# Causal linear attention in front of a mixture of experts: running sums of outer products replaced by chunks of 64 tokens

## What is computed

```python
Q, K, V = (proj(wq_w, wq_b), proj(wk_w, wk_b), proj(wv_w, wv_b))
scores = jnp.einsum('bhld,bhsd->bhls', Q, K)
causal = jnp.tril(jnp.ones((l, l), dtype=scores.dtype))
out = jnp.einsum('bhls,bhsd->bhld', scores * causal, V)
...
x = x + _L0_attn_ref(_layernorm(x, axis=-1), ...)
x = x + _L0_ffn_ref(_layernorm(x, axis=-1), ...)
```

## Time and profile before

| | |
|---|---|
| median of three executions | 309.36 us |
| profiled execution, first to last instruction | 350.7 us (no time outside the span is given for it) |
| busy: TensorE, VectorE, GpSimd, ScalarE | 234.8 (67%), 207.1 (59%), 198.4 (57%), 140.9 us (40%) |
| mean granted TensorE clock | 0.854 |
| chain that ended last | issue 52%, TensorE 27%, DMA 5%, SyncE's queue 4% |

### The profile page before, as it was taken

The page is one execution under the profiler, slowest core; times in us unless marked ns, Lnnn a source line. Parts: engine busy times, 40 slices in busy tenths (PEclk is TensorE's granted clock), DMA queues, the critical chain, the costliest instruction groups (busy, mean ns, idle before and its releaser), DMA issues.

```text
span 350.7 us, 6314 instructions
## 1 busy us (share of the span) xinstructions
PE 234.8 (67%) x1320; PEld 174.7 (50%) x1320; DVE 207.1 (59%) x745; ACT 140.9 (40%) x509; POOL 198.4 (57%) x184
## 2 busy tenths in 40 slices
PE   0799999999998999574300685977677686665000
PEld 0345666666565655363100675976567685554000
DVE  6888887989898989654541043434333443343074
ACT  2434566566565554342200363444343544342000
POOL 3465644588888888744673045554564455646300
PEclk9999999999999999855555599689898989999555
DMA  7910000000010101101121332223223232201199
GB/s 218 304 57 0 3 0 3 3 31 30 31 33 30 33 30 33 53 31 38 39 84 60 72 99 70 71 71 76 68 72 84 62 78 65 81 28 39 50 358 317
DMA packets 32399, 25.48 MB, mean 73 GB/s; under 512 B 4305, under 2 KB 30169, under 8 KB 32364
## 3 DMA queue, kind: packets, MB, share of 16 engines
q1 hardware_dynamic: 23808, 14.52, 15.2%
q0 software_dynamic: 4320, 8.47, 7.6%
q10 hardware_dynamic: 4236, 2.10, 2.0%
HBM read 13.92 MB, written 11.61 MB: 73 GB/s over the span
## 4 chain that ended last, share of the span: by engine, by line
issue 52%; PE 27%; DMA 5%; SPq 4%; ACT 3%; DVE 2%; ACTq 1%; another core or an unknown queue 1%; POOL 1%; DVEq 1%; POOLq 0%
PE ps L824 14%; PE ps L832 9%; PE ps L817 4%; DMA back<-returned 3%; ACT hT L458 3%; SPq L271 2%; SPq L289 2%; DMA bias_bc<-b_o 1%; DMA returned<-y_sb,xt 1%; POOL outer L324 1%; DMA xt<-dispatched 1%; DMA dispatched<-padding 1%; PE ps L709 0%; DVEq L243 0%
## 5 line engine op out<-in xcount | busy, mean ns | idle before, releaser
L349 POOL DMA_INDIRECT returned<-y_sb,xt x71 | 70.2, 988 | 70.9 <-DVE y_sb L685 51.3
L324 POOL TENSOR_TENSOR outer<-qkv 128x1024 f32<-128x1024 f32 x32 | 62.6, 1957 | 32.4 <-ACT qkv L404 32.0
L340 POOL DMA_INDIRECT dispatched<-rows,slot x64 | 62.5, 976 | 25.1 <-issue 15.4
L680 DVE TENSOR_TENSOR yb<-ps,b_bc 128x128 f32<-128x128 f32 x71 | 20.7, 291 | 77.2 <-PE ps L832 32.8
L824 PE MATMUL ps<-xT,w_of 128*128 128x128 f32 x284 | 51.1, 308 | 18.7 <-ACT hT L458 12.5
L739 PE MATMUL ps<-outer,causal 128*128 128x512 f32 x128 | 62.4, 610 | 0.0
L832 PE MATMUL ps<-w_sb,hT 128*128 x284 | 50.0, 304 | 16.3 <-ACT hT L458 10.3
L452 ACT ACTIVATE xT<-ps 128x128 f32<-128x128 f32 x71 | 19.8, 279 | 91.7 <-PE ps L817 72.1
L824 PEld LDWEIGHTS ps<-xT,w_of 128*128 128x128 f32 x284 | 42.8, 216 | 23.0 <-ACT xT L452 16.4
L832 PEld LDWEIGHTS ps<-w_sb,hT 128*128 128x128 f32 x284 | 42.3, 214 | 20.1 <-issue 19.9
L458 ACT ACTIVATE hT<-ps,b_col 128x128 f32<-128x128 f32 x142 | 44.4, 370 | 4.7 <-remote 3.0
(11 more groups left out here) (115 smaller groups left out, 355.5 us busy)
## 6 DMA issues: line engine op xcount, KB each, us to landing
xt<-dispatched SPq DMA_DIRECT2D x71, 65.0 KB
back<-returned SPq DMA_DIRECT2D x8, 512.0 KB, 7.6
x_sb<-x SPq DMA_DIRECT2D x8, 256.0 KB, 5.2
out<-x_sb ACTq DMA_DIRECT2D x8, 256.0 KB, 6.6
returned<-y_sb,xt POOLq DMA_INDIRECT x71, 2.3
w_sb<-w SPq DMA_DIRECT2D x1, 1024.0 KB, 5.6
w_sb<-w SPq DMA_DIRECT2D x2, 512.0 KB, 7.2
dispatched<-rows,slot POOLq DMA_INDIRECT x64
```

The source lines that it names most:

```text
L324: pool.tensor_tensor(outer[:, g % OUTER_RING, :].rearrange("p (h b a) -> p h b a", h=HEADS, b=DH), k, v, ALU.mult).then_inc(outer_done, 1)
L340: pool.indirect_dma_start(out=dispatched[:, :], out_offset=bass.IndirectOffsetOnAxis(ap=slot[:, g * K + k:g * K + k + 1], axis=0), in_=row ...
L349: pool.indirect_dma_start(out=returned[:, :], out_offset=bass.IndirectOffsetOnAxis(ap=xt[:, n % G, D:D + 1].bitcast(I32), axis=0), in_=y_s ...
```

## The change

The attention stage is replaced; the experts' stage and all that follows the count stay as they are.

- Tokens are taken in chunks of 64. Within a chunk the scores are formed and masked, between chunks a state is kept. The norm, both transposes, the projections, the copies and the gate run once a batch of four tiles, output, residual and second norm once for two tiles.
- `project_qk` gives q and k with the features on the partitions, 512 tokens at a time (L771, L773), with one PSUM bank for both; `project_kv` gives k and v with the tokens on the partitions in two halves that share a bank (L783, bias L785). ScalarE copies k (L383) and q (L401), and writes q four more times (L404), each with all but one head of every group of four set to zero (`member`, a 0/1 scale and bias per partition).
- `score_half` (L832): for each half of the heads, four matmuls of k's 32 feature rows and 64 tokens by q's four masked copies, 256 columns, into two partition halves and two banks. VectorE multiplies by the mask of the chunk (`mask_half`, L529, 512 columns).
- `within` (L848): eight matmuls of 64 token rows by 32 features of v, 256 columns. For each head of a group VectorE adds the wanted part (`member_step`, L550, four steps for two tiles, 256 columns).
- `sum_half`, `sum_tile` (L803, L793, L795): the state of each chunk, summed in PSUM; VectorE masks it (`state_out`, L523, 256 columns). `between` (L818): state by q, 64 columns for each chunk, copied by ScalarE (`between_out`, L422) to where the member steps add.
- GpSimd's outer product is gone; the constants that it wrote in its first slot come ahead. `zeros` is new there, and SyncE loads `bias_cols`. The statistics of the first norm move from ahead of VectorE's slots into them. `q_member`, `scores` and `state` lie in the tile `back`, which is otherwise used at the end.

```diff
-
-            def outer_product(g):
-                wait(pool, qkv_done, g + 1)
-                wait(pool, run_done, g + 1 - OUTER_RING)
-                k = heads(qkv[:, g % QKV_RING, D:2 * D]).unsqueeze(2).to_broadcast([P, HEADS, DH, DH])
-                v = heads(qkv[:, g % QKV_RING, 2 * D:3 * D]).unsqueeze(3).to_broadcast([P, HEADS, DH, DH])
-                pool.tensor_tensor(outer[:, g % OUTER_RING, :].rearrange("p (h b a) -> p h b a", h=HEADS, b=DH), k, v,
-                                   ALU.mult).then_inc(outer_done, 1)
...
-            tile_slots([(16, dispatch), (0, outer_product)], N)
+            tile_slots([(12, dispatch)], N)
...
+            def qT_out(g):
+                if g % T:
+                    return
+                b = g // T
+                wait(act, qT_mm, b + 1)
+                wait(act, between_mm, 2 * (b - 1))
+                act.activation(qT[:, b % 2, :], ps_qk, ACT.Identity, bias=bias_cols[:, 0:1]).then_inc(qT_done, 1)
+                act.wait_ge(bias_member_done, 1)
+                for m in range(M):
+                    act.activation(q_member[:, b % 2, m, :], ps_qk, ACT.Identity, bias=bias_member[:, m:m + 1],
+                                   scale=member[:, m:m + 1]).then_inc(qT_done, 1)
...
+            def kv_out(g):
+                if g % T:
+                    return
+                b = g // T
+                wait(act, within_mm, g - T)
+                wait(act, sum_mm, g - T)
+                for half in range(2):
+                    wait(act, kv_mm, 2 * b + half + 1)
+                    act.activation(kv[:, b % 2, 2 * half:2 * half + 2, :], ps_kv, ACT.Identity).then_inc(kv_done, 1)
...
+            def between_out(g):
+                if g % 2:
+                    return
+                wait(act, between_mm, g // 2 + 1)
+                wait(act, att_mm, g // 2 - 3)
+                act.activation(oT[:, g // T % 2, (g % T) * P:(g % T + 2) * P], ps_between, ACT.Identity).then_inc(between_done, 1)
...
-            tile_slots([(10, variance_log2), (12, exponentials), (10, scale2_out), (2, qkv_out), (11, xn2T_out), (1, xnT_out), (6, qT_out), (10, rows_out),
-                        (0, normalize), (7, oT_out), (0, deviations_ahead)], N)
+            tile_slots([(-6, deviation1), (4, deviation2), (-4, xnT_out), (8, exponentials), (1, between_out), (-3, kT_out),
+                        (-3, qT_out), (-2, kv_out), (4, rows_out), (-5, normalize), (7, xn2T_out)], N)
...
+            def state_out(g):
+                first = int(g % T == 0)
+                wait(dve, sum_mm, g + 1)
+                wait(dve, between_mm, g // 2 - 1)
+                dve.tensor_tensor(state[:, g % T, first:2, :], ps_sum[:, g // T % 2, first:2, :],
+                                  headmask[:, :].unsqueeze(1).to_broadcast([P, 2 - first, D]), ALU.mult).then_inc(state_done, 1)
...
+            def mask_half(g, half):
+                wait(dve, scores_mm, 2 * g + half + 1)
+                wait(dve, within_mm, g - 1)
+                dve.tensor_tensor(scores[:, g % 2, half * 2 * M * C:(half + 1) * 2 * M * C].rearrange("p (j m l) -> p j m l", j=2, m=M),
+                                  ps_scores.rearrange("p j (m l) -> p j m l", m=M),
+                                  chunk_causal[:, :].unsqueeze(1).unsqueeze(1).to_broadcast([P, 2, M, C]),
+                                  ALU.mult).then_inc(masked_done, 1)
...
+            def member_step(g, m):
+                if g % 2:
+                    return
+                b, pair = g // T, g // 2
+                if m == 0:
+                    wait(dve, within_mm, g + 2)
+                    wait(dve, between_done, pair + 1)
+                else:
+                    dve.wait_ge(member_out, (M - 1) * pair + m)
+                part = oT[:, b % 2, (g % T) * P:(g % T + 2) * P].rearrange("p (c f) -> p c f", c=2)
+                dve.scalar_tensor_tensor(out=part, in0=ps_o[:, m, :, :, :].rearrange("p c t l -> p c (t l)"), scalar=member[:, m:m + 1], in1=part,
+                                         op0=ALU.mult, op1=ALU.add).then_inc(oT_done if m == M - 1 else member_out, 1)
...
-            def attend(g):
-                wait(dve, run_done, g + 1)
-                wait(dve, qkv_done, g + 1)
-                wait(dve, o_done, g - 1)
-                q = heads(qkv[:, g % QKV_RING, 0:D]).unsqueeze(2).to_broadcast([P, HEADS, DH, DH])
-                run = ps_run[g % 2].rearrange("p u f -> p (u f)").rearrange("p (h b a) -> p h b a", h=HEADS, b=DH)
-                dve.tensor_tensor(prod[:, g % 2, :].rearrange("p (h b a) -> p h b a", h=HEADS, b=DH), run, q,
...
-
-            def attend_sum(g):
-                wait(dve, prod_done, g + 1)
-                wait(dve, oT_mm, g + 1 - RING)
-                dve.tensor_reduce(o_sb[:, g % RING, :], prod[:, g % 2, :].rearrange("p (f a) -> p f a", a=DH),
-                                  AX_X, ALU.add).then_inc(o_done, 1)
...
-            tile_slots([(6, stats2_out), (6, mean2_out), (5, add_residual), (9, softmax_end), (1, attend_sum),
-                        (8, softmax_start), (0, attend), (0, scales_ahead), (9, places), (6, shift2_out),
-                        (2, state_out)], N)
...
+            tile_slots([(11, places), (-5, shift1_out), (-5, constants), (2, member_0), (0, mask_0), (2, member_1), (3, add_residual),
+                        (8, softmax_start), (-6, mean1_out), (2, member_2), (3, stats2_out), (4, shift2_out), (0, mask_1),
+                        (2, member_3), (-1, state_out), (3, mean2_out), (9, softmax_end)], N)
...
+            def project_qk(g):
+                if g % T:
+                    return
+                b = g // T
+                wait(pe, xnT_done, b + 1)
+                wait(pe, between_done, 2 * b - 1)
+                pe.matmul(ps_qk, wqkv_sb[:, D:2 * D], xnT[:, b % 2, :], start=True, stop=True).then_inc(kT_mm, 1)
+                wait(pe, kT_done, b + 1)
+                pe.matmul(ps_qk, wqkv_sb[:, 0:D], xnT[:, b % 2, :], start=True, stop=True).then_inc(qT_mm, 1)
+
+            def project_kv(g):
+                if g % T:
+                    return
+                b = g // T
+                for half in range(2):
+                    wait(pe, kv_done, 2 * b + half)
+                    for u in range(2):
+                        at = 2 * half + u
+                        pe.matmul(ps_kv[:, u, :], xnT[:, b % 2, at * P:(at + 1) * P], wqkv_sb[:, D:3 * D], start=True, stop=False)
+                        wait(pe, bias_done, 4)
+                        mm = pe.matmul(ps_kv[:, u, :], ones[:, :], bias_parts[:, D:3 * D], start=False, stop=True)
+                    mm.then_inc(kv_mm, 1)
...
+            def sum_tile(g):
+                b, u = g // T, g % T
+                if u == 0:
+                    return
+                wait(pe, state_done, g)
+                pe.matmul(ps_sum[:, b % 2, 1, :], kv[C:P, b % 2, u - 1, 0:D], kv[C:P, b % 2, u - 1, D:2 * D],
+                          start=False, stop=True, skip_group_check=True).then_inc(half_mm, 1)
+                pe.matmul(ps_sum[:, b % 2, 0, :], kv[:, b % 2, u - 1, 0:D], kv[:, b % 2, u - 1, D:2 * D],
+                          start=False, stop=True, skip_group_check=True)
+
+            def sum_half(g):
+                b, u = g // T, g % T
+                wait(pe, kv_done, 2 * b + 2)
+                wait(pe, state_done, g)
+                wait(pe, half_mm, (T - 1) * b + u)
+                pe.matmul(ps_sum[:, b % 2, 1, :], kv[0:C, b % 2, u, 0:D], kv[0:C, b % 2, u, D:2 * D],
+                          start=(u == 0), stop=True, skip_group_check=True).then_inc(sum_mm, 1)
+
+            def between(g):
+                if g % 2:
+                    return
+                b = g // T
+                wait(pe, state_done, g + 2)
+                wait(pe, between_done, g // 2)
+                wait(pe, qT_done, (M + 1) * (min(b + 2, B) if g % T else b + 1))
                 for u in range(2):
-                    mm = pe.matmul(ps_run[g % 2][:, u, :], causal[:, :], outer[:, g % OUTER_RING, 512 * u:512 * (u + 1)],
-                                   start=True, stop=True)
-                mm.then_inc(run_done, 1)
...
+                        own = zeros[:, :] if g % T + u + c == 0 else state[:, g % T + u, c, :]
+                        if g == 0:
+                            pe.wait_ge(zeros_done, 1)
+                        mm = pe.matmul(ps_between[:, (2 * c + u) * C:(2 * c + u + 1) * C], own,
+                                       qT[:, b % 2, (g % T + u) * P + c * C:(g % T + u) * P + (c + 1) * C], start=True, stop=True)
+                mm.then_inc(between_mm, 1)
...
+            def score_half(g, half):
+                b, u = g // T, g % T
+                if u == 0:
+                    wait(pe, qT_done, (M + 1) * (b + 1))
+                    wait(pe, kT_done, b + 1)
+                wait(pe, masked_done, 2 * g + half)
+                for c in range(2):
+                    for j in range(2):
```

(25 more changed lines are left out.)

461 lines of the change are left out of this document (237 added, 224 removed).

## The result

The changed kernel takes **545.85 us** (median of four executions, 545.52 to 548.11) against 309.08 for the kernel before beside it: **1.767 times as long, interval 1.763 to 1.772**. The prediction was 480 with a range of 380 to 575. Direction and range held; 66 us are missing, and the sum comes out near by luck: two of its steps were wrong with opposite signs.

The account below looks back on a forecast made before the run. TensorE in the attention stage was taken as the bound. Eight batches of 28.1 us work plus 10.5 us waits give +183 us, start +5, tail -17: +171 on the 309.4 us median, so 480 us, range 380 to 575.

Parts of the forecast that it names:

- What bounds before, and that TensorE would get more work: Attention stage: TensorE, busy 120.9 of 126.1 us, is the bound; its work grows from 15.8 to 28.1 us a batch.
- A group of n then takes n + 1 passes: Scores and within-chunk products: the next small matmul starts only beside the previous one's second pass; 16.3 us a batch.
- the sign that I had set: Small matmuls in the attention stage: the forecast is wrong if their passes are shorter than 0.2 us.
- the rival of full overlap: Small-matmul groups: a group costs only two passes, 5.2 us a batch in all; 391 us, chance 0.20.
- Drain at 0.16 a change: Rival: TensorE waits 0.16 us at each of some 32 array-shape changes a batch; 521 us, chance 0.12.
- The other work, 11.8 us: TensorE's transposes, projections, state sums, between-chunk products, output, gate and ranking together take 11.8 us a batch.
- Waits, 10.5 us a batch: Attention stage: TensorE idles for VectorE's masks and states and ScalarE's copies, 10.5 us a batch.
- Half clock: Rival: TensorE's clock stays at 0.5 in the attention stage, 225 us more; 705 us, chance 0.04.
- Batch and sum: Attention stage: 28.1 us work plus 10.5 waits make 38.6 a batch, 309 for eight; whole kernel +171 us.
- first score at 24.4 and not 20: Kernel start: the first score comes at about 20 instead of 15.4 us, priced at +5 us.
- drain 17.3 and not 16: Tail of the last tiles up to the count: 16 us instead of 32.9, priced at -17 us.
- Not slower: Rival: full overlap also in the output's column halves and VectorE's answers hidden; 300 us, chance 0.07.

Follow-up runs that it names:

- e1_parts: Changed kernel plus bursts of independent f32 matmuls, on the whole array and on parts of it, ahead of TensorE's first slot; 677.5 us.
- e2_order: Changed kernel with VectorE's masks and states moved ahead of its member steps, residual and softmax; 539.4 us, 1.533 times before.
- e4_fill_small: Changed kernel plus useless bf16 matmuls on one 32x64 part of the array in TensorE's waits; 638.0 us, 1.811 times before.
- e8_whole_order: Changed kernel with whole-array bf16 matmuls replacing scores and within-chunk products, and VectorE's masks and states moved ahead of its other work; 402.3 us.
- e9_before_less: Kernel before plus useless whole-array matmuls: 16, 10 and 8 ahead of the last three rankings, 40 behind the count; 308.48 us against 309.58.
- e10_bursts: Changed kernel plus six pause-free matmul patterns ahead of its first slot, each entered at full clock behind 48 whole-array matmuls; 833.0 us.
- e3_fill: Changed kernel plus useless whole-array bf16 matmuls in TensorE's waits, 65 a batch; 524.1 us, 1.485 times before.
- e5_order_fill: Changed kernel with VectorE's masks and states moved earlier, plus useless whole-array bf16 matmuls on TensorE; 517.1 us, 1.471 times before.

## Why the prediction was right and where it was wrong

- **What bounds before, and that TensorE would get more work**: right. The stage is still TensorE's, VectorE and ScalarE have room, GpSimd's outer products were worth nothing.
- **"A group of n then takes n + 1 passes"**: wrong. 8 x 0.59 + 4 x 0.59 = 7.1 us a batch at the full clock instead of 16.3. I argued from the rows that the second pass of a matmul blocks the next; it blocks only its own part (`e1_parts`: 0.216 a pass on one part, 7 ns between starts on different ones). By the sign that I had set, passes of small matmuls under 0.2 us, the mechanism of my forecast is wrong. This was the rival of full overlap, which the two passes of 0.215 would have put at 5.2; the rest is the drain.
- **Drain at 0.16 a change**: right in kind and size (0.155), but it was a rival where it should have been a term: it holds together with full overlap.
- **The other work, 11.8 us**: near. Busy time of a steady batch is 40.2 us at half clock (109.22 x 50.2 / 136.5), so an estimated 20.1 at full; less 7.1 for the groups it leaves 13.0, changes of shape included. The estimate is a little low, since it halves all times, and a group of four goes from 1.06 to 0.59 only.
- **Waits, 10.5 us a batch**: right, and at the named places. Idle in the stage is 363.1 - 290.6 = 72.5, or 9.1 a batch (10.0 in a steady one). Changing VectorE's order alone (`e2_order`) gave back 62 us.
- **The clock**: the step that failed at the highest price. "Half clock" stood among the rivals at 0.04, on the ground that the expert stage has 0.89 with TensorE busy 72%. It came true, for all but 20.5 us of the stage, and cost some 20 us a batch. The rival's 705 us were too much mostly because it doubled 28.1 instead of 20.1. My evidence was the share of busy time; the runs show that this does not settle it: 98% busy at 0.50 (`e4_fill_small`), 91% at half rate (`e2_order`), 88% at a mean of 0.61 with whole-array matmuls in the groups (`e8_whole_order`).
- **Batch and sum**: 38.6 forecast, 50.2 steady, 45.4 on average (the first took 37.6 by its first scores, partly at full clock and with no gate or ranking yet). 8 x 45.4 - 309 = +54; first score at 24.4 and not 20, +4.4; drain 17.3 and not 16, +1. That is 60 of the 66. The rest most likely lies in my start: the profile of before comes from a slower chip and has the count at 174.4, where the profile of `e9_before_less`, from a quicker one and with its filler, has it at 166.7. So the +171 was laid on a start that is some 7 us shorter in the median.
- **"Not slower"**: excluded for a simple reason. Even with the scores and inner products left out for something shorter and most waits gone (`e8_whole_order`) the kernel takes 402 us. At the estimated 20.1 us of work a batch at the full clock and no wait at all, the stage would be 161 us against 126.

That the clock falls where TensorE runs whole-array work with pauses is shown by the start of the stage in `e10_bursts`; in the kernel after it had not come up before 55.7 us. Open is what separates a pattern that brings the clock back from one that doesn't more finely than these eight, why the same projections brought it back in some batches and not in others, and why it falls again in `e3_fill` after 65 us and in `e5_order_fill` after 99.

## What to carry to other kernels

Before cutting a matmul into small ones that need answers from another engine, price the clock: here both the pauses and what the array does between them decided whether it came back, and a busy TensorE at half rate looks the same in the busy column. Read the pitch of a known group at both levels and look for the place where the clock rises and falls. If answers of another engine are waited for, order that engine's queue by who waits (62 us here), and size filler for half the clock, so that it ends inside the wait.

## What the hardware showed unexpectedly

- The clock has memory. From 1.00, four-part and paired groups kept it through 14 us each (and 64-column, 64-row ones for 25 and 14.6); from 0.50 the same ones stayed there for 25 to 31 us. Whole-array streams of 128 columns rose after 5.4 us, full column halves after 4.35, and 32x64 matmuls in rotation over all eight parts after 3.8 (`e1_parts`).
- A change of the array's shape costs 0.155 us and a whole-array matmul does not overlap a small one: 4.70 us for 16 passes that are 3.46 in series.
- One 32x64 part used alone lost the clock after 3.0 us without a pause (`e1_parts`).
- The clock row reads 1.00 until the first recorded event, whatever the real rate. The window of `e2_order` below says 1.00 where a group of scores above starts at 154.14 and the next group 1.06 us later; pitch tells the truth there.

```profile
150.00:200.00 50.00, 45.09 (x248) 24.27 (x244) 19.09 (x70) 13.44 (x30) 7.75 (x8) 1.00 0.03 11
```
